# Graph attention on one core: edge steps of two slots instead of three, with VectorE's work of a step in a new order

## The reference

```python
# x (12500, 256), src and dst (200000,), dst sorted; 8 heads of 32
q = (h @ Wq.T + bq).reshape(N, HEAD_DIM, HEADS) * scaling
k = (h @ Wk.T + bk).reshape(N, HEAD_DIM, HEADS)
v = (h @ Wv.T + bv).reshape(N, HEAD_DIM, HEADS)
s = jnp.einsum('edh,edh->eh', q[row], k[col])      # row = src, col = dst
m = jax.ops.segment_max(s, row, num_segments=N)
e = jnp.exp(s - m[row])
z = jax.ops.segment_sum(e, row, num_segments=N)
attn = e / z[row]
out = jax.ops.segment_sum(attn[:, None, :] * v[col], row, num_segments=N)
x = _layernorm(x + (out.reshape(N, -1) @ Wo.T + bo))
```

## Time and profile before

| | us |
|---|---|
| median of 3 runs | 4021.01 (4016.24 to 4050.6) |
| profiled execution, its own time | 4017.71 |
| its span, first to last instruction | 4015.6 |
| DVE busy | 3211.0 (80%) |
| POOL busy | 2447.6 (61%) |
| PE busy / weight loads | 2227.2 (55%) / 1514.8 (38%) |
| ACT busy | 1504.6 (37%) |

### The profile page before, as it was taken

One profiled execution on the slowest core, in us unless ns is written; L12 is line 12 of the kernel. 1 busy time (PEld: TensorE's weight loads), 2 busy tenths in 40 slices (PEclk: granted clock), 3 DMA queues, 4 the chain that ended last, 5 costly groups with the idle time before them and its releaser, 6 DMA issues. The chain is left out here.

```text
span 4015.6 us, 59591 instructions
## 1 busy us (share of the span) xinstructions
PE 2227.2 (55%) x7109; PEld 1514.8 (38%) x7109; DVE 3211.0 (80%) x8164; ACT 1504.6 (37%) x6480; POOL 2447.6 (61%) x2365
## 2 busy tenths in 40 slices
PE   3999888653002555555555545555555555544776
PEld 3788775432001333333333333333333333323443
DVE  8554467799223999999999999999999999977776
ACT  0110002221001555555555555555555555534332
POOL 3221120003767777777777777777777777765677
PEclk9966568776555788778777787777877778766777
DMA  1211013226513788878887887888777788799222
GB/s 33 64 58 32 16 43 101 89 67 125 171 36 96 231 233 232 232 232 232 231 232 232 232 232 231 232 232 231 232 232 231 232 232 232 229 177 169 80 92 85
DMA packets 329217, 665.86 MB, mean 166 GB/s; under 512 B 63462, under 2 KB 191750, under 8 KB 329016
## 3 DMA queue, kind: packets, MB, share of 16 engines
q0 software_dynamic: 160768, 518.27, 46.4%
q1 hardware_dynamic: 168392, 146.96, 12.7%
HBM read 599.35 MB, written 65.86 MB: 166 GB/s over the span
## 5 line engine op out<-in xcount | busy, mean ns | idle before, releaser
L931 POOL DMA_INDIRECT kv<-kv_rows,idx x1794 | 1863.0, 1038 | 583.7 <-issue 538.5
L1032 PE MATMUL sum_ps<-pv,ident 128*128 128x264 f32 x2392 | 902.0, 512 | 1299.3 <-DVE pv L825 1299.3
L1032 PEld LDWEIGHTS sum_ps<-pv,ident 128*128 128x128 f32 x2392 | 511.3, 237 | 1712.1 <-DVE pv L825 1393.1
L987 ACT ACTIVATE pv<-kv,s 128x33 f32<-128x33 f32 x4784 | 1084.4, 309 | 53.9 <-ACT s L977 27.3
L790 DVE TENSOR_TENSOR prod<-kv,q 128x768 f32<-128x768 f32 x598 | 569.2, 952 | 59.7 <-DMA kv<-kv_rows,idx 59.6
L797 DVE TENSOR_REDUCE s<-prod 128x24 f32<-128x768 f32 x598 | 565.5, 946 | 0.0
L977 ACT ACTIVATE s<-s 128x32 f32<-128x32 f32 x598 | 137.0, 229 | 1126.1 <-DVE s L818 1126.1
L1034 PE MATMUL sum_ps<-pv,ident 128*128 128x264 f32 x1196 | 497.3, 508 | 0.0
L507 PE MATMUL hist_ps<-hot_lo,hot_hi 125*98 125x128 bf16 x1600 | 372.1, 409 | 121.7 <-DVE hot_hi L174 121.7
L825 DVE TENSOR_TENSOR pv<-kv,s 128x528 f32<-128x528 f32 x598 | 417.4, 698 | 0.3 <-ACT s L977 0.3
L507 PEld LDWEIGHTS hist_ps<-hot_lo,hot_hi 125*98 125x98 bf16 x1600 | 370.3, 259 | 123.2 <-issue 68.7
(11 more groups left out here) (164 smaller groups left out, 2450.5 us busy)
## 6 DMA issues: line engine op xcount, KB each, us to landing
q<-q_perm SPq DMA_DIRECT2D x598, 128.0 KB, 3.7
kv<-kv_rows,idx POOLq DMA_INDIRECT x1794, 4.0
kv_rows<-kv_st SPq DMA_DIRECT2D x98, 260.0 KB, 3.0
xt_sb<-in_xT SPq DMA_DIRECT2D x98, 128.0 KB, 3.2
node_rows<-q_st SPq DMA_DIRECT2D x98, 128.0 KB, 3.4
q_perm<-kv_st SPq DMA_DIRECT2D x98, 128.0 KB, 1.9
kv_st<-node_rows,node_id POOLq DMA_INDIRECT x98, 3.1
cols<-edge_keys,run_at POOLq DMA_INDIRECT x98, 2.5
```

The source lines that it names most:

```text
L931: pool.indirect_dma_start(out=kv[:, j, g, :], out_offset=None, in_=kv_rows, in_offset=bass.IndirectOffsetOnAxis(ap=idx[:, j, g:g + 1], axi ...
L987: last = act.activation(pv[:, b, V * VW + at_h:V * VW + at_h + HD + 1], kv[:, j, V, D + at_h:D + at_h + HD + 1], ACT.Copy, scale=s[:, b, V ...
L1032: pe.matmul(sum_ps[b][:, 0:VW], ident[:, :], pv[:, b, g * VW:(g + 1) * VW], start=g == 0, stop=False)
```

## The change

Steps have two slots instead of three, so 849 steps instead of 598, and `V` is 1: DVE weighs one slot, ACT the other. `C` is 40. The order of `step` is new: the look-up stands first, `add_sum` comes before `weigh`, the copy of the old maximum is a function of its own ahead of `weigh`, and `scale_acc` stands between the mask and the maxima. The planning tables of the layout stage move from `pv` and `prod` to `kv`, where they have room.

```diff
-G = 3
+G = 2
-C = 39
+C = 40
...
-        room = pv[:, :, :].rearrange("p b w -> p (b w)")
-        step_f, past, tile_f = room[:, 0:STEPS], room[:, STEPS:2 * STEPS], kv[0:1, U - 1, :, :].rearrange("p g w -> p (g w)")[:, 0:STEPS]
-        place_f = prod[0:1, :, :].rearrange("p g d -> p (g d)")[:, 0:STEPS]
+        room = kv[:, :, :, :].rearrange("p u g w -> p (u g w)")
+        step_f, past = room[:, 0:STEPS], room[:, STEPS:2 * STEPS]
+        tile_f, place_f = room[0:1, 2 * STEPS:3 * STEPS], room[0:1, 3 * STEPS:4 * STEPS]
...
-                def mask_scores(k, b, col, tile):
+                def old_maximum(k, b, tile):
 
                     dve.tensor_copy(s[:, b, G * HEADS:], runmax[:, bass.ds(tile * HEADS, HEADS)]).then_inc(old_copied, 1)
+
+                def mask_scores(k, b, col):
+
                     dve.wait_ge(scored, k + 1)
...
                     b, b1 = j % 2, (j + 1) % 2
-                    score_sum(k + 1, b1, peeled=peel and j == 0)
-                    weigh(k, j % U, b, peeled=peel and j < 2)
-
                     tile, tile1, col1 = (bounded(dve, tile_r[j % 3], TILES), bounded(dve, tile_r[(j + 1) % 3], TILES),
                                          bounded(dve, col_r[(j + 1) % 3], TAB * C - G))
                     before = None if peel and j == 0 else bounded(dve, tile_r[(j + 2) % 3], TILES)
                     look_up(k + 2, (j + 2) % 3)
-                    mask_scores(k + 1, b1, col1, tile1)
-                    maxima(k + 1, b1, tile1)
+                    score_sum(k + 1, b1, peeled=peel and j == 0)
                     if before is not None:
                         add_sum(k - 1, b1, before)
+                    old_maximum(k + 1, b1, tile1)
+                    weigh(k, j % U, b, peeled=peel and j < 2)
+                    mask_scores(k + 1, b1, col1)
+                    scale_acc(k, b, tile, first=peel and j == 0)
+                    maxima(k + 1, b1, tile1)
                     if not last:
                         score(k + 2, (j + 2) % U, turn + (j + 2) // U)
-                    scale_acc(k, b, tile, first=peel and j == 0)
                     differences(k + 1, b1, tile1)
```

More of the change, by code:

```diff
@@ L880, in _ @@
                 tile, col = bounded(dve, tile_r[0], TILES), bounded(dve, col_r[0], TAB * C - G)
-                mask_scores(0, 0, col, tile)
+                old_maximum(0, 0, tile)
+                mask_scores(0, 0, col)
                 maxima(0, 0, tile)
```

## The result

The changed kernel takes 4398.76 us (median of 4 runs, 4398.64 to 4400.74), the kernel before 4022.43 in the same comparison: ratio 1.092, 95% interval 1.087 to 1.097. It is slower, as forecast, but by 376 us and not by 646: the time lies 41 us under the stated range. Times here are medians of all runs, while ratios compare only runs in the faster of two states, since the kernels with three slots at times run slower (the kernel before took 4010 to 4204 us in all its runs).

The account below looks back on a forecast made before the run. DVE was taken to pace the loop, GpSimd close behind. 813 steps at 3.63 us (2951), masked steps 137 and 12 at the end gave 3100 against 2455 us: plus 647, predicted 4668 us, range 4440 to 4790.

Parts of the forecast that it names:

- A: Sequencer not held, look-up hidden under score and differences; TensorE's ring at 1.2 GHz sets 3.2 us, about 4320 us; chance 0.09.
- B: Sequencer not held, TensorE at 2.4 GHz long enough: step 2.87 us, about 4050 us, not slower; chance 0.04.
- The new DVE step: DVE's starts from score_sum: end of maxima at 2.13 us, step 2.85 us if the next score_sum followed at once.
- The moved look-up: Sequencer between maxima and score_sum: 1.28 us plus 0.15 preparation, DVE idle about 0.6 us; step 3.63 us with the branch.
- The branch: Loop's end on the sequencer, hidden before, exposed after: 0.4 us per six steps, 0.07 us a step.
- Masked steps: 36 steps on the masked tile, bound by reading one row repeatedly: 3.8 us each by traffic, 137 us in all.
- The range: 4440 to 4790 us; step bounds 3.41 to 3.78 us give 4490 to 4790; leaves out three rivals, 2 in 10.
- What lies beside it: GpSimd's gathers (2.67 us), traffic, ACT (2.3 us) and TensorE all fit within the 3.63 us step.
- TensorE's ring: Addition, copy, weigh, four TensorE passes, semaphore back: 3.2 us at 1.2 GHz; 0.4 us spare in the forecast's step.
- the two chains: Sequencer's look-up before score_sum (step 3.63 us, chance 0.80) and TensorE's ring (3.2 us, rival A, 0.09).

Follow-up runs that it names:

- a single fix: Changed kernel without the look-up in its steps, 4320.0 us, or with two extra matmuls a step, 4378.8 us; both at once, 3834.2 us.
- the same two fixes: Changed kernel, complete, with the look-up in two parts, 4351.1 us, or with two extra matmuls, 4378.8 us; both at once, 4031.2 us.
- the kernel with a step of 2.88 us: Changed kernel with the look-up in two parts (read behind weigh), one extra matmul and masked rows spread: 4009.4 us, ratio 0.994.
- the one with 3.09: Changed kernel with masked rows spread, one extra matmul, table read ahead of score_sum and taken apart behind weigh: 4183.0 us.

## Why the prediction was right and wrong

**The direction and its cause: right.** The term that I called decisive, the look-up in front of score_sum, is the one that the rows show. The sequencer passes differences only when maxima has ended, does the whole look-up, and score_sum starts behind it; the kernel with a second table read shows it from the other side (0.65 us more work, 0.65 us more per step). The Trainium skill's "Perfetto Trace Analysis", section "DVE / Act Engine Instruction", by which the sequencer is free once a waiting instruction is in the wait queue, gave rivals A and B; the register operation at 2402.3, 47 ns after the end of maxima and 0.47 us before differences starts, goes against it for this sequence of instructions.

**The step that failed: the size of the step, 3.63 us against 3.33.** Two terms of "The new DVE step" and "The moved look-up" were too long, by about the same.
- The end of maxima was put at 2.13 us after score_sum; it is at 1.96 (maxima 2405.35 + 0.17 = 2405.52, less 2403.56). I had taken the distances between starts from pairs of the old order. Several of them were not DVE's own: copy to the next instruction was put at 0.15 and is 0.07, mask to the next at 0.14 and is 0.09, maxima itself at 0.20 and is 0.17; maxima to the next, 0.22 in the forecast and 0.10 now, moves only score and differences. In the old order the sequencer was in the way: in the step of the earlier trace rows the mask starts 47 ns and the addition 46 ns after the end of a register operation of its own. A distance between two starts that holds such a wait can't be carried over to another order. Why the maxima take 0.17 us is not shown.
- From the end of maxima to score_sum I had 1.43; it is 1.28. The register operation in front of score_sum (45 ns) is not there any more, and the look-up's last one takes 151 ns instead of 242.

The branch came out as forecast: the step with the loop's end is 0.46 us longer (0.08 per step, 0.07 said). Together the step is 0.30 us shorter than said, which times 813 is 244 us of the 270 that the forecast was too high.

**Masked steps:** 3.8 us each were expected from the traffic; the 38 scorings between 3970 and 4100 us stand 3.42 apart, 14 us less in all. That the steps of the kernel before are slow there because of the one row is now shown by the run with 128 rows.

**The range: wrong.** I bounded the step below at 3.41 by hiding single pieces of the look-up, and left DVE's own 2.13 without a bound; that was the term with the worse evidence.

**What lies beside it: right by luck in one place.** I gave TensorE's ring 0.4 us of spare time. Against a step of 3.63 us that would have been so; against the real one there is none, and it did no harm to the forecast only because the ring is not longer than the other chain. Rival A's ring, put at 3.2, is 3.25, and its clock (TensorE stays at 1.2 GHz) is what happened: 0.50 in every window. A was wrong only in that the look-up would cost nothing: its time, about 4320 us, is that of the kernel without the look-up (4320.0). I had priced the two chains as alternatives, but each alone is enough for 3.25 us.

**Two slips that moved nothing.** ScalarE's pieces add up to 2.23 us and not 2.3; and the copy is not the instruction with the longest gap before it, since maxima starts 0.13 us after the mask's end and the copy 0.06 after weigh's.

**Not the slots as such:** the number of steps, the second scaling of the accumulator and the q rows make 849 steps cost as much DVE work (3241 us) as 598 did (3211.0). What the change paid for is the hole in front of score_sum.

## What to carry to other kernels

In these kernels DVE's register work (a table look-up, a snapped index, a loop's branch) starts only when the instruction ahead of it has got its semaphore; it costs nothing only if the engine has that much work already handed over. So before cutting a loop into shorter steps, compare its register work in one piece (1.2 us here) with the work that the engine has in hand at that place (0.7 us of score and differences behind the end of the maxima). And before taking away the wait that a profile shows, measure the next chain: here a single fix gave 79 or 20 us, both 565, though in kernels that leave the look-up out; in a complete kernel the same two fixes gave 48 and 20, together 368.

## What was not expected of the hardware

**A gather waits for a VectorE instruction that reads two SBUF tensors.** The timeline of the kernel with spread rows and a divided look-up, one gather in the middle of a multiplication, and one that isn't:

```profile
2401.58 0.99 POOL L937 DMA_INDIRECT kv<-kv_rows,idx  x1 [0.30 <-issue]
...
2402.50 0.96 DVE L790 TENSOR_TENSOR prod<-kv,q 128x768 f32<-128x768 f32 x1 [0.42 <-DMA kv<-kv_rows,idx]
...
2402.88 1.45 POOL L937 DMA_INDIRECT kv<-kv_rows,idx  x1 [0.30 <-issue]
```

The multiplication ends at 2403.46, the gather 0.87 us later, at 2404.33; a free gather takes 0.99. Counted in this trace from 1500 to 3400 us:

- 312 of 1,305 gathers start within a score multiplication, and their mean is 1.50 us; 161 start within weigh, which also reads two tensors in SBUF, with a mean of 1.23; 274 start within score_sum, which reads one, with a mean of 1.00.
- All 412 that start at least 0.08 us into score or weigh, and at least 0.15 before its end, end 0.87 or 0.88 us after it.
- The 353 that start in the last 0.15 us before such an instruction take 1.00 us, at most 1.01. So only the gather's start collides; once begun, it runs through.

The kernel before has a mean of 1.03, since its gathers start beside the sum, beside or behind the maxima, or, 395 of 474 times, in the last 0.2 us of the multiplication. So the old loop ran well by a favourable phase between DVE (4.01 us a step) and three gathers, which take as long. That the edit lost this phase by moving DVE's instructions is argued from these counts; no run tests it by itself. The Trainium skill's "SBUF — State Buffer", section "Who interferes with whom", says that a tensor_tensor with both inputs in SBUF contends with GpSimd's reads; these rows agree, and show it for indirect gathers.

**TensorE's granted clock with extra matmuls.** Two more matmuls a step, whose result nobody reads, took the granted clock from 0.50 to 1.00 in the changed loop. With one more it was 1.00 in the kernel with a step of 2.88 us, and 0.94 in the one with 3.09.
